# Carrying the value blocks through DRAM instead of transposing them on TensorE, with new orders of work and moved loads

## The reference, cut to what matters

```python
x = L0_attn_q                                   # (1, 1024, 512)
xn = _layernorm(x, axis=-1)
qkv = xn @ w_qkv.T                              # 32 query heads, 8 key and 8 value heads of 128
scores = einsum('bskgd,btkd->bkgst', qh, kh) / sqrt(128); causal mask; probs = softmax(scores)
s = einsum('bkgst,btkd->bskgd', probs, vh).reshape(...) @ w_dense.T
h = relu(s0 * xn @ W0) * 2;  h = relu(ei(h, W1)) * 2;  g = silu(ei(h, W2))   # W = +1 or -1 of a boolean
return x + s * g
```

## Time and profile before

| | |
|---|---|
| median of three runs | 911.28 us |
| the profiled execution | 912.8 us, of which the span of the profile is 910.6 |
| busy: PE, PEld, DVE, ACT, POOL | 98%, 83%, 73%, 57%, 51% of the span |
| granted TensorE clock, mean | 0.998 |
| one pass through the loop body (third of seven) | 105.2 us |
| DMA traffic | 143.83 MB in 204980 packets |

### The profile page before, as it was taken

The page is one execution under the profiler, slowest core; times in us unless marked ns, Lnnn a source line. Parts: engine busy times, 40 slices in busy tenths (PEclk is TensorE's granted clock), DMA queues, the critical chain, the costliest instruction groups (busy, mean ns, idle before and its releaser), DMA issues.

```text
span 910.6 us, 16004 instructions
## 1 busy us (share of the span) xinstructions
PE 896.6 (98%) x4299; PEld 758.9 (83%) x4299; DVE 667.0 (73%) x1162; ACT 520.2 (57%) x1096; POOL 465.5 (51%) x372
## 2 busy tenths in 40 slices
...
PEclk9999999999999999999999999999999999999999
...
GB/s 185 160 207 231 141 108 143 240 160 133 85 208 213 167 121 114 219 192 122 108 178 219 159 149 79 206 219 151 115 112 267 142 131 100 150 143 148 104 141 148
DMA packets 204980, 143.83 MB, mean 158 GB/s; under 512 B 23168, under 2 KB 172416, under 8 KB 204928
## 3 DMA queue, kind: packets, MB, share of 16 engines
q1 hardware_dynamic: 176256, 129.68, 57.0%
q10 hardware_dynamic: 28672, 13.64, 6.7%
...
## 4 chain that ended last, share of the span: by engine, by line
issue 42%; POOL 28%; PE 27%; DMA 1%; ACT 1%; DVE 1%; POOLq 1%; SPq 0%; DVEq 0%
POOL pt_lo L787 21%; POOL w_lo L799 4%; PE ps_m L1161 4%; PE ps_m L1162 4%; PE ps_m L1163 4%; PE ps_m L1322 3%; POOL wd_lo L799 3%; PE ps_o L1161 2%; PE ps_o L1163 2%; PE ps_o L1162 2%; PE ps_s L1162 2%; PE ps_s L1163 2%; PE ps_s L1161 2%; PE ps_s L1307 2%; DMA raw<-wqkv 1%
## 5 line engine op out<-in xcount | busy, mean ns | idle before, releaser
L787 POOL TENSOR_TENSOR pt_lo<-pt_lo,pt_hi 128x512 fp32r<-128x512 f32 x248 | 327.5, 1345 | 285.7 <-ACT pt_hi L909 285.7
L1004 DVE CUSTOM_DVE_ANT_0 ps_s<-ps_s,mask 128x32 f32<-128x32 f32 (+31 forms) x256 | 182.3, 713 | 116.9 <-PE ps_s L1163 115.8
L909 ACT ACTIVATE pt_hi<-pt_lo 128x512 fp32r<-128x512 f32 x288 | 169.4, 625 | 53.3 <-PE ps_o L1163 34.9
L1161 PE MATMUL ps_m<-xn_hi,w_hi 128*128 128x512 f32 (+1 forms) x392 | 153.8, 392 | 2.9 <-POOL w_lo L799 1.8
L1162 PE MATMUL ps_m<-xn_lo,w_hi 128*128 128x512 f32 (+1 forms) x392 | 151.8, 387 | 0.0
L1163 PE MATMUL ps_m<-xn_hi,w_lo 128*128 128x512 f32 (+1 forms) x392 | 151.6, 387 | 0.0
L1163 PE MATMUL ps_s<-k_hi,q_lo 128*128 128x480 f32 (+15 forms) x384 | 126.9, 331 | 0.0
L1162 PE MATMUL ps_s<-k_lo,q_hi 128*128 128x480 f32 (+15 forms) x384 | 126.9, 331 | 0.0
L1161 PE MATMUL ps_s<-k_hi,q_hi 128*128 128x480 f32 (+15 forms) x384 | 125.0, 326 | 1.6 <-ACT prob_even L853 1.6
L853 ACT ACTIVATE prob_odd<-ps_s,small 128x160 f32<-128x160 f32 (+15 forms) x128 | 96.1, 754 | 42.3 <-DVE small L1004 36.3
L853 ACT ACTIVATE prob_even<-ps_s,small 128x32 f32<-128x32 f32 (+15 forms) x128 | 82.4, 644 | 64.9 <-DVE small L1004 63.0
(11 more groups left out here) (105 smaller groups left out, 1456.4 us busy)
## 6 DMA issues: line engine op xcount, KB each, us to landing
...
```

The costliest lines, as they stand in the source:

```text
L787: pool.tensor_tensor(pt_lo[:, slot, :], pt_lo[:, slot, :].bitcast(F32), pt_hi[:, hi_slot, :], ALU.subtract).then_inc(land_lo, 1)
L909: act.activation(pt_hi[:, hi_slot, :], pt_lo[:, LAND_AT[i] + j, :].bitcast(F32), ACT.Copy).then_inc(land_hi, 1)
L1004: dve.tensor_tensor_reduce(out=scores, in0=scores, in1=mask[:, S - width(i % BLOCKS, tile):S], scale=-1.0, scalar=BIG, op0=ALU.add, op1=AL ...
L1161: pe.matmul(out, sta_hi, mov_hi, start=start, stop=False)
```

## The change

The TensorE item `vblocks` goes away. DVE now takes v out of PSUM with its own transpose of 32x32 squares into `vt`. SP writes `vt` to a DRAM tensor `values` in 4 DMAs (`vw.HALF`) with runs of 32 floats, and reads it back in one DMA into `v_lo` (`vr.HALF`), which puts the squares in their places. ACT copies `v_hi` from there and POOL, not DVE, subtracts. `weigh.0.0` and `weigh.4.4` wait for that.

```diff
@@ vector engine
-                            dve.tensor_copy(vt[:, :], bank[:, :]).then_inc(shared_read, 1)
+                            if kind != "prologue":
+                                dve.wait_ge(v_written, 16 * CHUNKS * (r.value_writes(half) - 1))
+                            dve.transpose(vt[:, :], bank[:, :]).then_inc(shared_read, 1)
-                    elif name == "vblocks":
-                        dve.wait_ge(shared_hi, r.hi_no(item))
-                        dve.tensor_tensor(v_lo[...], bank[:, :]..., v_hi[...], ALU.subtract)
@@ sync engine
+                    elif what == "vw":
+                        sp.wait_ge(shared_read, r.shared_no(("unit", "v", half)))
+                        for n in range(CHUNKS):
+                            sp.dma_start(values_d[half, :, :, :, n, :].rearrange("j b a c -> a (j b) c"),
+                                         vt[n * Q:(n + 1) * Q, :].rearrange("a (n c) -> a n c", c=Q))\
+                              .then_inc(v_written, 16)
+                    elif what == "vr":
+                        sp.wait_ge(v_written, 16 * CHUNKS * r.value_writes(half))
+                        if kind != "prologue":
+                            sp.sem_inc(v_seen)
+                            sp.wait_ge(block_weighed, WEIGHED0 + PAIRS * g + (0 if half else pair_no(7, 3) + 1))
+                        sp.dma_start(v_lo[:, half * 4:half * 4 + 4, :].bitcast(F32),
+                                     values_d[half, ...].rearrange("j b a q c -> (b a) j (q c)")).then_inc(v_landed, 16)
@@ scalar engine
-                        act.wait_ge(shared_done, r.shared_no(item))
-                        act.activation(v_hi[...], bank[:, :]..., ACT.Copy).then_inc(shared_hi, 1)
+                        act.wait_ge(v_landed, 16 * r.value_no(half))
+                        act.activation(v_hi[:, rows, :], v_lo[:, rows, :].bitcast(F32), ACT.Copy).then_inc(v_hi_done, 1)
@@ gpsimd
+                        pool.wait_ge(v_hi_done, r.value_no(half))
+                        pool.tensor_tensor(v_lo[:, rows, :], v_lo[:, rows, :].bitcast(F32), v_hi[:, rows, :],
+                                           ALU.subtract).then_inc(v_split, 1)
@@ tensor engine
-                    elif name == "vblocks":
-                        for n in range(4):
-                            mm = pe.transpose(bank[:, n * P:(n + 1) * P], vt[:, n * P:(n + 1) * P], ident[:, :])
-                            pe.wait_ge(shared_read, r.shared0)
+                            pe.wait_ge(v_split, r.value_no(0))
```

```diff
-WARM_BETWEEN = 14
+WARM_BETWEEN = 12
-LOAD_X_BEFORE = {0: (0, 1, 2, 3), 2: (4, 5), 3: (6, 7)}
+LOAD_X_BEFORE = {0: (0, 1), 2: (2, 3), 3: (4, 5), 4: (6, 7)}
-    act = [("root_table",)] + root[:1] + hi(split[0], split[1], *ln(0, 1)) + ...
+    act = [("root_table",)] + hi(split[0]) + root[:1] + hi(*ln(0, 1), split[1]) + ...
```

All orders of the body and of the last part are new. Two pieces of TensorE's table for the body, before (minus) and now (plus), from `weigh.6.4` on:

```diff
-        unit.q1.0.3 unit.k.0.0 unit.k.0.1 weigh.6.6 unit.k.0.2 weigh.6.5 weigh.6.4 unit.k.0.3
-        unit.q2.0.0 unit.q2.0.1 unit.q2.0.2 unit.q2.0.3 dense.4.0 dense.4.1 weigh.6.3 dense.4.2
-        weigh.6.2 scores.8.0 weigh.6.1 dense.4.3 weigh.6.0 dense.5.0 dense.5.1 dense.5.2 dense.5.3
-        scores.8.1 unit.v.0.0 scores.8.2 unit.v.0.1 unit.v.0.2 weigh.7.0 weigh.7.1 unit.v.0.3
-        weigh.7.2 weigh.7.3 scores.8.3 weigh.7.4 weigh.7.5 weigh.7.6 weigh.7.7 vblocks.0 dense.6.0
+        unit.k.0.2 weigh.6.6 unit.k.0.3 weigh.6.5 weigh.6.4 unit.q0.0.0 unit.q0.0.1 weigh.6.3
+        unit.q0.0.2 unit.q0.0.3 unit.q3.0.0 unit.q3.0.1 unit.q3.0.2 unit.q3.0.3 dense.4.0
+        dense.4.1 weigh.6.2 dense.4.2 scores.8.0 dense.4.3 weigh.6.1 weigh.6.0 scores.8.1
+        dense.5.0 scores.8.2 dense.5.1 dense.5.2 weigh.7.0 weigh.7.1 dense.5.3 weigh.7.2 weigh.7.3
+        scores.8.3 weigh.7.4 weigh.7.5 weigh.7.6 weigh.7.7 dense.6.0 dense.6.1 dense.6.2 dense.6.3
```

More of the change, by code:

```diff
@@ L129, in has_hi @@
 def has_hi(item):
-    return item[0] in ("vblocks", "hidden") or (item[0] == "unit" and item[1] != "v")
+    return item[0] == "hidden" or (item[0] == "unit" and item[1] != "v")
 def parse(tokens):
@@ L149, in prologue @@
     ln = lambda *blocks: [("ln", b) for b in blocks]
-    values = [("vblocks", 0)]
     tiles = range(TILES)
@@ L153, in prologue @@
     pe = ln(0, 1) + [("warm",), ("begin", "q0")] + ln(2, 3) + [("begin", "q1")] + unit("q0")[-1:] + unit("q1")[-1:] + unit("q2") \
-        + unit("q3") + ln(4, 5) + unit("k") + ln(6, 7) + unit("v") + [("scores", first, r) for r in tiles] + values
+        + unit("q3") + ln(4, 5) + unit("k") + ln(6, 7) + unit("v") + [("scores", first, r) for r in tiles]
     units = [("unit", p, 0) for p in ("q0", "q1", "q2", "q3", "k", "v")]
@@ new lines @@
+        exp.3.0 hi.unit.q2.1 exp.3.1 exp.3.2 hi.weigh.0 hi.unit.q0.1 hi.split.q0 exp.3.3
+        hi.unit.q1.1 hi.split.q1 hi.split.q2 hi.split.q3 hi.land.1.0 hi.land.1.1 hi.split.k
+        exp.4.0 exp.4.1 hi.land.2.0 hi.land.2.1 exp.4.2 hi.land.2.2 hi.weigh.1 exp.4.3 exp.5.0
+        amove.4.0 hi.split.v hi.unit.q2.0 amove.4.1 amove.4.2 amove.4.3 exp.5.1 hi.land.3.0
+        hi.land.3.1 hi.land.3.2 hi.land.3.3 exp.5.2 hi.weigh.2 exp.5.3 hi.vblocks.1 hi.unit.q1.0
+        hi.land.4.0 hi.land.4.1 hi.land.4.2 hi.land.4.3 amove.5.0 exp.6.0 hi.land.4.4 amove.5.1
@@ L215 @@
+        exp.8.3 hi.weigh.7
     """,
     "dve": """
[L217 to L221 removed]
@@ new lines @@
+        flip.5.0 flip.5.1 flip.5.2 max.6.0 flip.5.3 max.6.1 mul.weigh.3 lo.unit.q1.0 inverse.5
+        max.6.2 max.6.3 lo.weigh.3 lo.dense.2 flip.6.0 flip.6.1 max.7.0 max.7.1 flip.6.2
+        lo.unit.v.0 flip.6.3 mul.weigh.4 max.7.2 lo.weigh.4 max.7.3 lo.dense.3 inverse.6 flip.7.0
+        flip.7.1 lo.land.6.4 flip.7.2 lo.unit.k.0 lo.land.6.1 mul.weigh.5 flip.7.3 lo.weigh.5
+        lo.unit.q0.0 inverse.7 lo.unit.q3.0 max.8.0 lo.dense.4 mul.weigh.6 max.8.1 max.8.2
+        lo.land.7.1 lo.weigh.6 lo.land.7.4 lo.dense.5 max.8.3 lo.land.7.7 flip.8 inverse.8
@@ L308 @@
-        lo.land.7.7 gate.5 mul.weigh.7 lo.weigh.7 gate.7
+        max.1.0 max.1.1 max.1.2 max.1.3 max.2.0 max.2.1 max.2.2 max.2.3 flip.1 lo.unit.q1.1
+        inverse.1 flip.2 lo.unit.q2.1 max.3.0 inverse.2 max.3.1 lo.unit.q0.1 max.3.2 mul.weigh.0
+        max.3.3 lo.weigh.0 lo.unit.q3.1 flip.3 lo.unit.k.1 inverse.3 lo.unit.v.1 max.4.0 max.4.1
+        max.4.2 max.4.3 lo.dense.0 flip.4.0 max.5.0 lo.hidden.0.0.0 max.5.1 flip.4.1 flip.4.2
+        mul.weigh.1 lo.hidden.0.0.1 flip.4.3 lo.weigh.1 lo.hidden.0.0.2 mul.weigh.2 inverse.4
@@ L309 @@
+        lo.hidden.1.1.0 lo.hidden.1.1.1 lo.hidden.1.1.2 lo.land.7.1 lo.hidden.1.1.3 mul.weigh.6
+        gate.0 lo.weigh.6 gate.1 gate.2 lo.land.7.4 gate.3 gate.4 lo.land.7.7 gate.5 mul.weigh.7
+        lo.weigh.7 gate.7
         lo.dense.6 add_x.7 gate.6 lo.dense.7
@@ L339, in shared @@
     return [whole(i) for i in ORDERS[kind]["pe"]
-            if i[0] == "vblocks" or (i[0] in ("unit", "dense", "hidden") and i[-1] == CHUNKS - 1)]
+            if i[0] in ("unit", "dense", "hidden") and i[-1] == CHUNKS - 1]
 PRO_SHARED, BODY_SHARED = len(shared("prologue")), len(shared("body"))
@@ L788, in run @@
                                            pt_hi[:, hi_slot, :], ALU.subtract).then_inc(land_lo, 1)
+                    elif what == "lo" and item[0][0] == "vblocks":
+                        half = item[0][1]
+                        rows = slice(half * 4, half * 4 + 4)
+                        pool.wait_ge(v_hi_done, r.value_no(half))
+                        pool.tensor_tensor(v_lo[:, rows, :], v_lo[:, rows, :].bitcast(F32), v_hi[:, rows, :],
+                                           ALU.subtract).then_inc(v_split, 1)
                     elif what == "lo":
```

280 lines of the change are left out of this document (134 added, 146 removed).

## The result

The kernel after the change takes 917.9 us (median of 7 runs, 916.8 to 921.1), the kernel before 911.5 (7 runs on the same chip): ratio 1.0073, 95% interval 1.0059 to 1.0087. So it is **slower by 6.6 us** by the ratio (6.4 between the medians), where 3.3 us faster was forecast. The profiled execution after took 918.36 us, span 916.5.

The account below looks back on a forecast made before the run. TensorE's own work, busy 98% of the span, was taken to set the time. Terms 6.6 - 4.8 - 0.7 + 2.2 gave 3.3 us less, median 911.3 to 908.0 us; range 901.5 to 915.

Parts of the forecast that it names:

- Part 1: Transposes leaving TensorE: 0.44 us for each of 15 vblocks, 6.6 us less in all.
- lower bound: DVE's transpose of v from PSUM: 0 to 0.7 us longer than its 684 ns copy, nearest to 0.
- Part 2: End of body: row 7's moves and POOL pieces unchanged, TensorE one triple shorter; 7 x 0.68 = 4.8 us given back.
- part 3: Middle of body: row 4's moves have less room, stall 0.1 us at weigh.4.0 over seven passes, 0.7 us lost.
- the slower rival: Values' writes and read delay row 4's moves; at upper-bound packet cost 1.5 us stall per pass, 917.8 us; chance 0.18.
- ACT's order: Copy of unit.q1.0 on ACT ahead of row 4's piece: stall of 0.1 to 0.2 us at weigh.4.0.
- the upper bound of 6.0: Values' 2048 packets per half at 47 ns: 6.0 us of all DMA engines; lower bound 1.1, taken 2.5.
- my 15.0 us: TensorE's own work from the gate of row 4's moves to weigh.4.0, where it was 16.3 us.
- Part 4: Prologue and first pass: 2.2 us less, bounds 0 and 5.0; row 1's writes may hold the first pass.
- entry wait and slow clock: Body's entry: body starts 1.8 us sooner; 1.7 us lost to slow clock goes if idle time goes.
- "same": Chance 0.22 that measurement can't be told from no change (0.2%, 1.8 us); faster 0.58, slower 0.20.

Follow-up runs that it names:

- e6: The change with the old orders for body and last part (values by DRAM, new prologue), and weigh.3.0 one triple later on TensorE; 907.6 us, ratio 0.9972.
- e9: e6 with the loads of q2 and q3 moved on SP behind row 1's writes; 908.0 us, ratio 0.9974 to the kernel before.
- e4: The kernel before with the new prologue alone, transposes and orders of before; 908.65 us, ratio 0.9984.
- e11: e9 with the values' writes ahead of the output-weight loads and two of these loads behind row 4's moves; 906.2 us, ratio 0.9959.
- e8: e4 with the loads of q2 and q3 moved on SP behind row 1's writes; 907.5 us, ratio 0.9973.
- e12: e2 with the first of row 7's pieces (land.7.0) subtracted by DVE, not POOL; 909.4 us, ratio 0.9986.
- e13: e11 with the first of row 7's pieces (land.7.0) subtracted by DVE, not POOL; 912.1 us, ratio 1.0027.
- e14: e4 with the change's new orders of body and last part, values still transposed by TensorE and none in DRAM; 915.2 us, ratio 1.0047.
- e2: The kernel after with the values' read and the last output-weight load moved behind row 4's moves in the body; 911.5 us, ratio 1.0008.
- e7: The kernel after with the four output-weight loads moved behind row 4's moves in the body; 910.3 us, ratio 0.9997.
- e3: The kernel after with the values' DMAs in body and last part carrying a sixteenth of the bytes, same issues; 909.9 us, ratio 0.9989.

## Why the prediction was wrong

**Part 1 held as a size.** The transposes leave TensorE's list: the best passes of e6 and e9 take 104.1 us where e4 has 105.1, and 2 x 0.44 = 0.88 was the forecast. The means of their passes 2 to 7 are 104.8 and 104.6, since other waits take a third to two thirds of it back. DVE's copy of v out of PSUM (0.68 us) became a transpose of 0.72 us, near the lower bound. The Trainium skill (VectorE: DVE Perf Modes, Rules for kernel authors) advises to leave 128x128 transposes to TensorE if PSUM will do. For the change as it was made that was right. With the orders mended it isn't decided: e11, by DRAM, has 0.9959, e8, with transposes, 0.9973, and their intervals overlap. The 390 ns of the Trainium skill (VectorE: DVE Perf Modes, The three transpose paths) are for bf16. Taken as an occupation they would have made 23 us, and the earlier trace rows puts them at 6.6. What decides is not the price of either path but what the other path does to the queue.

**Part 2 held, in place and size.** Behind the gate every kernel with the values in DRAM (e12 and e13 apart), whether with 26 or 27 triples there, takes 27.0 us when undisturbed; with transposes 27.4. So the chain sets it (e12 shows it by shortening it, by half of what was expected), and the triple that the new orders put ahead of the gate is lost. e14 gives the new orders 5.7 us; my terms were 4.8 here and 0.7 in part 3. In passes 2 to 7 it is 1.0 us each: 0.68 for the triple and 0.3 for the gap at weigh.4.0. The wait came in two pieces, 0.47 at weigh.7.0 and 0.24 at weigh.7.6 in the third pass, with small ones between.

**Part 3 is the step that failed.** I wrote that row 4's moves "land about when ACT comes to them" and took 0.1 us a pass. Measured in the profile after: 0.67 us of marked waits on average in passes 2 to 7, and 1.59 in the first pass; the sign that I had set for the slower rival, above 0.5 us at weigh.4.0, was there. The gap, marked or not, was 0.86 us a pass. 0.3 of that is ACT's order, which I had as 0.1 to 0.2; the rest is the late landing. The edits that take the late landing away gave 5.9 us (e2), 6.9 (e7) and 7.7 (e3), the first pass included.

How the landing came about can be read, from one profiled execution of each kernel, by setting side by side how far row 3's read stood ahead of row 4's moves (passes 2 to 7) and the moves' median landing:

| kernel | read ahead of the moves | landing |
|---|---|---|
| before | 10.5 to 10.9 us | 2.2 |
| e14, new orders, no values in DRAM | 4.8 to 5.0 | 2.4 |
| e3, the values' issues with a sixteenth of the bytes | 2.8 to 3.0 | 4.3 |
| after | 2.1 to 3.0 | 5.8 |

In the last three, passes 2 to 7, the moves are issued 34.3 to 35.1 us into the pass. The late read and the 1 MB of weights alone, as in e14, do no harm. The four writes of values take SP 2.5 us and push the read 2 us towards the moves: 1.9 us later landing. Their bytes and those of the read add 1.5. So the values' DMAs cost 3.4 us of landing, where I had 2.5: I counted the writes' packets (3.0 for writes and read by e3, and the upper bound of 6.0 is refuted), but not the read of 256 KB, and not SP's time as something that moves the 1 MB read behind it. I had the order of SP's list in front of me and didn't work out its times. Nor do the moves start at TensorE's gate, as my 15.0 us assumed: SP waits for DVE's flip, 0.8 us in e14's third pass, so there was less room than I had.

The slower rival had the right place and the right cause, the values' writes and read in front of the moves; its price, by packets, was wrong, and its time (917.8 against 917.9) is right by accident: the stall is half as long as its 1.5 us, and the first pass gives the rest. It had 0.18 and should have been first.

**Part 4 was right for the prologue and wrong for the first pass.** e4 gives 1.4 us for the prologue alone (interval 0.6 to 2.4), within my bounds and near the 2.2; entry wait and slow clock went as said. But I let the values' DMAs cost nothing there except delay for row 1. In after, 111.3 us against e4's 107.5, they join the clearing of `y`, the loads and row 1's writes, and TensorE has three waits of 1.3 to 1.6 us that it hadn't before. e14's first pass, with the new orders and no values in DRAM, takes 106.2; e7's, with the values but the weights out of the way, 107.5. That points to the sum again. But the waits at weigh.3.0 and weigh.7.0 there were not followed to their cause, one execution of each kernel was profiled, and with the values the first pass varies from 105.9 to 111.9 over e9 to e12; its share of each edit's gain stays open.

**The sum again, by the ratios:** new prologue -1.4 (e4), new orders +5.7 (e14 against e4), the values' way by DRAM +2.4 (after against e14), in all +6.7. The last is the 6.6 of the transposes against 9.0 of waits. My sum had nothing for it; it is the failed step, and its like in the first pass. The traces of after and e14, each transpose counted, give 637.9 - 636.6 + 6 x 0.88 = 6.6 in passes 2 to 7 and 111.3 - 106.2 + 0.9 = 6.0 in the first, less 1.4 before and behind them: 11.3 in all. Of the 6.6, row 4's late landing is 6 x 0.56 = 3.4 (gaps of 0.86 against 0.30), and 2.2 come behind the gate, where after waits 0.3 to 0.9 us at weigh.7.0 in four passes. After's profiled execution lies 0.5 us above its median and e14's 0.5 below; the remaining 1.3 us between 11.3 and 9.0 are within the intervals of the two ratios.

One slip in my sum of chances: by its own rule "same" gets 0.40 / 6 + 0.22 x 4 / 5 = 0.24 and slower 0.18, not 0.22 and 0.20.
